# Second attention of a two-layer decoder: the loop over its eight sequences written out for all engines

## What is computed

```python
kqv = x @ W_kqv + b_kqv                      # x: (8, 512, 256) after the layer norm
k, q, v = split(kqv, 3), each (8, 512, 16, 16)
attn = einsum('bqhd,bkhd->bhqk', q, k) / sqrt(16)
bias = slopes[:, None, None] * tril(j - i), -1e30 where j > i
attn = softmax(attn + bias)
y = einsum('bhqk,bkhd->bqhd', attn, v).reshape(b, s, e)
x = x + y @ W_proj + b_proj
```

## Time and profile before

| | |
|---|---|
| median of 3 runs | 2821.2 us |
| profiled execution | 2796.56 us |
| its span | 2794.8 us |
| TensorE busy | 83% of the span |
| VectorE busy | 43% |
| ScalarE, GpSimd busy | 24%, 20% |
| mean granted TensorE clock | 0.896 |

### The profile page before, as it was taken

The page is one execution under the profiler, slowest core; times in us unless marked ns, Lnnn a source line. Parts: engine busy times, 40 slices in busy tenths (PEclk is TensorE's granted clock), DMA queues, the critical chain, the costliest instruction groups (busy, mean ns, idle before and its releaser), DMA issues. The chain is left out here.

```text
span 2794.8 us, 36200 instructions
## 1 busy us (share of the span) xinstructions
PE 2324.2 (83%) x10514; PEld 1614.7 (58%) x10515; DVE 1212.4 (43%) x3389; ACT 672.5 (24%) x1269; POOL 550.4 (20%) x748
## 2 busy tenths in 40 slices
PE   5887676650799956887877896988999999999998
PEld 3554344450477734444544553777677777777776
DVE  3442788661233345655554652545432222222234
ACT  1211233310111122433433442212122122222221
POOL 1110233227000032332332221001430000000043
PEclk9997899855899976888887988996999999999999
DMA  6000000042122223333233210003520101101033
GB/s 212 0 0 19 1 0 0 23 151 103 59 64 65 64 60 84 77 73 73 50 73 71 61 39 18 5 26 131 184 68 31 34 30 33 34 30 34 28 91 94
DMA packets 122391, 160.27 MB, mean 57 GB/s; under 512 B 21106, under 2 KB 90546, under 8 KB 122034
## 3 DMA queue, kind: packets, MB, share of 16 engines
q1 hardware_dynamic: 110002, 125.53, 16.0%
q0 software_dynamic: 12288, 33.57, 3.8%
HBM read 75.68 MB, written 49.28 MB: 45 GB/s over the span
## 5 line engine op out<-in xcount | busy, mean ns | idle before, releaser
L1437 PE MATMUL e_up_ps<-e_wgu,e_xT 128*128 x1152 | 344.9, 452 | 0.0
L2030 DVE CUSTOM_DVE_ANT_0 a_s_ps<-a_s_ps,a_causal 128x512 f32<-128x512 f32 (+3 forms) x512 | 241.4, 515 | 174.2 <-PE a_s_ps L1815 132.3
L1543 DVE TENSOR_TENSOR e_h<-e_act_g,e_up_ps 128x344 f32<-128x344 f32 x208 | 106.6, 513 | 475.5 <-PE e_ht_ps L1444 438.7
L1954 ACT ACTIVATE a_prob<-a_st_ps 128x512 f32<-128x512 f32 (+1 forms) x384 | 198.1, 523 | 357.3 <-PE a_st_ps L1832 354.5
L1437 PEld LDWEIGHTS e_up_ps<-e_wgu,e_xT 128*128 128x128 f32 x1152 | 218.9, 190 | 103.7
L1470 ACT ACTIVATE e_act_g<-e_up_ps 128x344 f32<-128x344 f32 x208 | 95.2, 457 | 674.6 <-DVE e_h L1543 451.5
L1815 PE MATMUL a_s_ps<-a_ks,a_qs 68*128 68x512 f32 (+3 forms) x512 | 165.1, 392 | 91.3 <-DVE a_most L2030 78.9
L1832 PE MATMUL a_st_ps<-a_qs,a_ks 128*128 128x512 f32 (+3 forms) x512 | 197.3, 437 | 11.8 <-DMA a_qs<-a_m_lo 8.6
L1453 PE MATMUL e_y_ps<-e_wd,e_hT 128*128 x864 | 198.4, 379 | 0.0
L1392 POOL DMA_INDIRECT e_wgu<-slots_y,slot x64 | 61.0, 954 | 657.2 <-DMA slots_y<-e_y 609.7
L1721 POOL TENSOR_SCALAR_AFFINE_SELECT a_prob<-a_prob 128x256 f32<-128x256 f32 x256 | 101.2, 420 | 425.5 <-ACT a_prob L1954 425.3
(11 more groups left out here) (384 smaller groups left out, 3779.7 us busy)
## 6 DMA issues: line engine op xcount, KB each, us to landing
e_xin<-slots_x SPq DMA_DIRECT2D x144, 128.0 KB, 2.0
slots_y<-e_y SPq DMA_DIRECT2D x144, 128.0 KB, 1.7
slots_x<-zero_row SPq DMA_DIRECT2D x1, 9216.0 KB, 27.0
e_w<-in_L_ffn_w SPq DMA_DIRECT2D x16, 512.0 KB, 9.8
a_qs<-a_hi SPq DMA_DIRECT2D x32, 256.0 KB, 4.6
a_ks<-a_hi SPq DMA_DIRECT2D x32, 256.0 KB, 5.1
a_qs<-a_lo SPq DMA_DIRECT2D x32, 256.0 KB, 6.2
a_ks<-a_lo SPq DMA_DIRECT2D x32, 256.0 KB, 7.2
```

Of the source, the lines that this page charges most:

```text
L1437: last = pe.matmul(up_ps[:, 2 * half_ + u_, 0:H], xT[:, j, k * P:(k + 1) * P], up[:, k, u_, half_ * H:(half_ + 1) * H], start=k == 0, stop ...
L1543: dve.tensor_tensor(h[:, half_ * H:(half_ + 1) * H], act_g[:, :], up_ps[:, 2 * half_ + 1, 0:H], ALU.mult).then_inc(h_kept, 1)
L1954: act.activation(prob[:, gr % 2, u // 3, (u % 3) * BANK:(u % 3) * BANK + cols], st_ps[:, u % 2, 0:cols], ACT.Exp).then_inc(exp_done, 1)
L2030: last = dve.tensor_tensor_reduce(s_ps[:, u % 2, off:off + cols], s_ps[:, u % 2, off:off + cols], causal[:, S - cols:], 1.0, -3.0e38, ALU. ...
```

## The change

The helper loses its loop. It calls the body eight times with plain numbers, so each engine's program of this stage holds eight copies of the body where it held four, and every count and every address is a constant. The order of the work, the tiles and the transfers stay as they are.

```diff
-def over_sequences_ahead(eng, body):
-
-    body(0, 1, 2)
-    with eng.Fori(1, B - 2) as b:
-        body(b, b + 1, b + 2)
-    body(B - 2, B - 1, None)
-    body(B - 1, None, None)
+def over_sequences_ahead(body):
+
+    for b in range(B):
+        body(b, *(b + n if b + n < B else None for n in (1, 2)))
...
-            over_sequences_ahead(sp, body)
+            over_sequences_ahead(body)
```

More of the change, by code:

```diff
@@ L1783, in body @@
                         norm.gpsimd(following)
-            over_sequences_ahead(pool, body)
+            over_sequences_ahead(body)
         @block.tensor
@@ L1922, in body @@
                         score_by_key(b, gr, u)
-            over_sequences_ahead(pe, body)
+            over_sequences_ahead(body)
             for t in range(TB):
@@ L2006, in body @@
                             high_qk(nxt, 2 + (1, 9).index(u))
-            over_sequences_ahead(act, body)
+            over_sequences_ahead(body)
             keep_outputs(B - 1, G - 1)
@@ L2142, in body @@
                         stats(following)
-            over_sequences_ahead(dve, body)
+            over_sequences_ahead(body)
             normalise(B - 1, G - 2)
```

## The result

The changed kernel takes 2752.7 us (median of 4 runs, 2746.05 to 2756.91), the kernel before beside it 2822.3 (4 runs, 2819.69 to 2829.18). The ratio is 0.9748, with a 95% interval of 0.972 to 0.9775: 69.6 us less. The forecast was 2760, with a range of 2744 to 2788.

What follows compares the result with a forecast made beforehand. It took TensorE, busy 83% of the span, to bound the kernel, with VectorE's idles at loop jumps on its path. Gains of 59.3 and 1.5 us off the median 2821.2 gave 2760 us, range 2744 to 2788.

Steps and rivals of the forecast that it cites:

- Where the loss lay: Layer 1's second attention, sequences 2 to 5: 69.1 us lost, about 56 around VectorE's jumps from loop end to head.
- the prediction's last part: Expected profile: no 5 us VectorE idles, sequences 1 to 6 at 66 to 69 us, first quarters near 16.
- The jump's removal, 59.3 us: Sequences 2 to 5 without the jump back: 334.07 us falls by 59.3, bounds 40.5 to 69.1.
- 60.8 us in all: Whole predicted gain: 59.3 us for the jump back and 1.5 us for register arithmetic.
- The term for clock dips, 9.8 us: Sequences 2 to 5: each charged 2.45 us for a lower TensorE clock, 9.8 us off the 69.1 us gain.
- Register arithmetic, 1.5 us: Wait counts worked out at run time on VectorE, five passes: constants gain 1.5 us, bounds nothing to 3.2.
- More code, nothing; "ten or so" packets: Longer programs, 1020 more instructions on TensorE: ten or so more queue 8 packets in sequences 2 to 5, costing nothing.
- The rival that ended slower: TensorE's written-out code: about ten fetches of 5.1 us stop it while VectorE keeps its idles, 2872 us; chance 0.03.
- The base: Whole kernel: profiled 2796.6 us gave a sum of 2735.8; the same 60.8 off the median 2821.2 gave 2760.4.
- The clock takes part of it back: Rival: sequences 2 to 5 go as 0 and 7 do, at lower TensorE clock; gain 40.5, 2779 us; chance 0.15.
- Half of the idles stay: Rival: one of two VectorE idles stays in each of sequences 2 to 5 through late fetches; 2788 us; chance 0.04.

Runs made afterwards that it cites:

- set C: Third session of runs, on one chip: the changed kernel again and straight code with registers, beside the kernel before, which took 2823.1 us (11 runs).
- sets A and C: Two of three sessions of runs, each on one chip beside the kernel before, which took 2823.8 us in A (13 runs) and 2823.1 in C (11 runs).
- slot 100: Kernel before, loop kept on all engines, VectorE's loop head placed at slot 100 of a block of 256 instructions: 2808.5 us, ratio 0.9941.
- slot 230: Kernel before, loop kept, VectorE's loop head placed at slot 230 of a block of 256 instructions: 2792.8 us, a single execution.
- set B: Second session of runs, on one chip, each compared with the kernel before, which took 2797.7 us there (19 runs).

## Why the prediction was right

*Where the loss lay.* Right, with its mechanism. VectorE alone straight gives everything and the rest gives nothing. In the changed kernel's first profile all first quarters are near 16 us at a clock of 1.00, the long idles are gone from the maxima, and sequences 1 to 6 take 65.8 to 68.1 us, as the prediction's last part asked. In the second profile three of them take 72.4 to 72.7 us at a clock of 0.88, beyond what it allowed. What the experiments show is the jumps on VectorE and that a hint given ahead takes their idles away; that each idle is a fetch is the only reading found that fits both, but no row shows the fetch.

*The jump's removal, 59.3 us.* The first profile gives 334.07 - 266.42 = 67.7, the second (set C) 334.07 - 279.59 = 54.5. The prediction's 4 x 68.70 = 274.8 lies between them, and so do its 60.8 us in all between the two measured differences of medians, 69.6 and 2823.1 - 2766.0 = 57.1. The term for clock dips, 9.8 us over four sequences at full clock, was 266.42 - 4 x 65.86 = 3.0 in the one and 16.2 in the other. It was sized well on average, but it is no constant: it is the part that makes the two profiles differ most. That it came out near the middle of the two is partly luck: it was one sequence's dip, charged four times.

*Register arithmetic, 1.5 us.* Full-clock sequences take 65.84 to 65.88 now and took 66.25: 0.4 us each, 1.9 us for five. Right within what can be read at full clock; in the time it can't be seen. The 66.25 us of sequence 1, from which the prediction took what a pass without a jump costs, is the lowest of eight such profiles with registers on VectorE; that it still led to the right size is luck, since constants brought the sequences near it.

*More code, nothing; "ten or so" packets.* 42 became 52, and the run with only VectorE straight, which leaves queue 8 at 42, is as fast. So the packets are TensorE's, as the prediction took them to be. The rival that ended slower had this as its mechanism, and no idle of 5 us ahead of a matmul appeared.

*The base.* The sum against the profiled execution, 2735.8, came out at 2746.05, 10 us off in the other direction from the median. The step that did not hold is that it took the profiled 2796.6 and the median 2821.2 to differ by something that stays equal on both sides of the change. The last stretches took 21 us more in the profile after, as in sets A and C. That the 60.8 us were then taken off the median, and not off the profile, kept the number right: the executions of before beside the changed kernel (2819.7 to 2829.2) are at the level that goes with slow last stretches, so by this reading both sides had them.

*The rivals.* "The clock takes part of it back" (2779) is not the median of either measurement, but one execution of the changed kernel took 2777.8: it describes the slow end of the spread. "Half of the idles stay" is what slot 100 made: one idle of two stayed, and it gave 15 us, far less than half, since one stop costs the first quarter 9 to 12 us where two cost 12 to 15. At 2788 that rival was too cheap; by this run it would have been near 2806.

## What to carry to other kernels

Where an engine idles some 5 us behind a loop's back edge with nothing released, count its instructions in a pass. The table of waits (issue), the sequencer's branch row and the row of the loop's first instruction show it. Here 300 instructions on VectorE sufficed, on an engine busy 43%, and the price was 69 us for 41 us of idle (57 and 53 in the other two sets), because TensorE waited and lost its clock. Writing the loop out on that engine alone is enough; a hint keeps the loop and got 41 of the 69. Read a small gain only at equal granted clock, in windows cut at the same instructions, and with more than one profile.

## What I had not expected of the hardware

- A loop in two neighbouring blocks still paid one stop of 5.3 us a pass (slot 100), and the branch that enters the loop from ahead of it paid one too (slot 230, 5.34 us).
- Delays of 10.1 us a sequence as ordinary work cost nearly as much as the two stops (49.9 against 52.6 us in set B): the size of the loss is TensorE's, not the fetch's.
- The last two stretches of the kernel took 282.6 to 282.9 us in one set (and 282.55 in the profile of the kernel before that the prediction was made from) and 303.4 to 308.9 in two others, the same instructions with 188 to 189 and with 166 to 169 GB/s in the first of them. No run tried the cause; two of the sets carry the same chip number and differ.
- A straight sequence without a stop took 65.9 to 72.7 us in two profiles of one program, and of what was read only TensorE's busy time and granted clock (1.00 to 0.88) tell them apart.
